# Row lists of a mixture of experts: tokens outside an expert numbered from the end, twelve of sixteen tiles listed in the first part

## The reference

```python
logits = tokens @ router_weight.T + router_bias        # 2048 tokens, 8 experts
top, experts = top_k(logits, 4); share = softmax(top)  # 4 experts for each token
for e in range(8):                                     # rows = the tokens that chose e
    gate, up = rows @ gate_up_proj[e].T + gate_up_bias[e]
    y = (limited up + 1) * glu(gate) @ down_proj[e].T + down_bias[e]
    out[rows] += share[rows, e] * y
```

## Time and profile before

| | |
|---|---|
| median of 3 runs | 985.96 us (985.22 to 992.37) |
| profiled execution | 991.85 us, of which 990.1 us from its first to its last instruction |
| mean granted TensorE clock | 0.880 |
| PE, DVE, ACT, POOL busy | 82%, 64%, 50%, 29% of the span |
| first part | ends at 617.3 us of the span |
| second part | 617.8 to 990.1 us |

### The profile page before, as it was taken

How to read it: one execution, slowest core, us unless ns; L and a number is a source line. 1 busy time by engine, 2 the same in 40 slices (tenths; PEclk the granted TensorE clock), 3 DMA queues, 4 the chain that set the end, 5 groups by cost and what they waited for, 6 DMA issues and landing times. The chain is left out here.

```text
span 990.1 us, 18525 instructions
## 1 busy us (share of the span) xinstructions
PE 808.7 (82%) x6324; PEld 508.7 (51%) x6324; DVE 634.9 (64%) x1238; ACT 493.2 (50%) x950; POOL 286.3 (29%) x261
## 2 busy tenths in 40 slices
PE   0682776778876888987887798899999999999993
PEld 0341332233432434432242225489899989998993
DVE  4546657787678876886779932845666666665652
ACT  1210310454353553436548572157777777777772
POOL 6005002210040100001001000236666666666643
PEclk9796688759997997987867799789999999999997
DMA  8421362014230161102544311314444444444432
GB/s 279 115 67 57 110 182 79 32 44 129 49 113 33 37 194 34 49 23 96 178 144 139 120 64 43 109 34 66 67 67 66 66 67 67 66 67 66 65 47 32
DMA packets 72072, 83.22 MB, mean 84 GB/s; under 512 B 10288, under 2 KB 65200, under 8 KB 71856
## 3 DMA queue, kind: packets, MB, share of 16 engines
q1 hardware_dynamic: 57008, 61.25, 20.3%
q0 software_dynamic: 14976, 20.78, 13.0%
HBM read 52.71 MB, written 29.29 MB: 83 GB/s over the span
## 5 line engine op out<-in xcount | busy, mean ns | idle before, releaser
L1600 PE MATMUL gu_ps<-xt,w 128*128 128x256 f16 x1872 | 219.6, 275 | 1.2 <-ACT xt L1321 1.2
L672 ACT ACTIVATE p<-st 128x512 f32<-128x512 f32 x256 | 139.1, 597 | 137.9 <-PE st L1156 137.1
L883 DVE TENSOR_REDUCE neg_max<-sc 128x2 f32<-128x1024 f32 x128 | 156.5, 1222 | 61.9 <-PE sc L1132 60.6
L1600 PEld LDWEIGHTS gu_ps<-xt,w 128*128 (+1 forms) x1872 | 182.6, 99 | 23.6 <-issue 1.9
L1391 POOL DMA_INDIRECT out<-y,block_rows x78 | 125.4, 1608 | 103.4 <-ACT y L1351 83.0
L1614 PE MATMUL dn_ps<-w,h 128*128 (+1 forms) x936 | 108.6, 273 | 0.3 <-DVE h L1518 0.3
L1383 POOL DMA_INDIRECT gx<-xr_d,block_rows x78 | 86.0, 1102 | 51.5 <-DVE block_rows L1491 28.6
L1132 PE MATMUL sc<-kz,sq 48*128 48x512 f16 x256 | 61.9, 453 | 45.9 <-DVE neg_max L883 41.4
L1614 PEld LDWEIGHTS dn_ps<-w,h 128*128 128x128 f16 x936 | 91.5, 98 | 11.2 <-issue 0.6
L580 POOL COPY rden_rows<-rden 128x512 f32<-128x512 f32 x16 | 10.7, 668 | 282.3 <-DVE rden L904 250.1
L1509 DVE TENSOR_SCALAR up<-up 128x512 f32<-128x512 f32 x78 | 33.4, 428 | 83.0 <-ACT up L1337 82.9
(11 more groups left out here) (200 smaller groups left out, 1108.6 us busy)
## 6 DMA issues: line engine op xcount, KB each, us to landing
stack_d<-t SPq DMA_DIRECT2D x16, 256.0 KB, 2.4
raw<-in_gate_up_t SPq DMA_DIRECT2D x4, 1024.0 KB, 5.2
raw_next<-in_gate_up_t SPq DMA_DIRECT2D x4, 1024.0 KB, 5.5
sq<-stack_d SPq DMA_DIRECT2D x16, 192.0 KB, 3.6
kz<-stack_d SPq DMA_DIRECT2D x16, 192.0 KB, 4.7
sq<-stack_d SPq DMA_DIRECT2D x32, 96.0 KB, 2.4
kz<-stack_d SPq DMA_DIRECT2D x32, 96.0 KB, 2.3
ctx_pad<-in_ctx SPq DMA_DIRECT2D x4, 512.0 KB, 4.3
```

Source lines behind the costliest of these rows:

```text
L672: act.activation(p32[:, n // 2 % RING, 2 * (n % 2) + i, :], st[:, i, :], ACT.Exp, scale=QSCALE).then_inc(s_exp, 1)
L883: dve.tensor_reduce(neg_max[:, qt, :, pair], sc[:], AX.X, ALU.max, negate=True).then_inc(m_max, 1)
L1600: ins = pe.matmul(gu_ps[:, 2 * half + g, q * ROWS:(q + 1) * ROWS], weights(i, wi, slice(col, col + P)), xt[:, i % 2, kd, xi, :], start=(j ...
```

## The change

Tokens outside an expert are now numbered from the end of the 2048 places: such a token's place is 2047 minus the number of unchosen tokens ahead of it, and that needs no count of the expert. `behind` holds the token's number minus 2047. All places can be made before the later tiles are chosen, so the lists of the first twelve tiles (`FIRST` = 12) are made in the first part, in seven new steps of batch 3. The last four tiles (`T` = 4) stay in the second part. `base` holds the counts of the first twelve tiles; `take_rows` adds the two lists. `chosen` becomes float16, and the constants come in one transfer `list_no` of 128 x 3456 float16 (864 KB) into `raw`, once the weights of expert 6 are split. In the first part `low_hot` has room for four experts (`LOW_HOT`), in `raw_next`, so the step `list_low(7)` waits for the matmuls `list_rows(3)`. In the second part the transfers `high_no` and `low_no` (512 KB each) are gone, all experts' lists are listed ahead of `gate_up(0, 0)`, and DVE does the last `take_rows` and `list_rows` 2 to 4 ahead of `unit(0)`. The fillers ahead of the last `den`, `den_turn` and `o_proj` are gone; other counts of fillers are cut. `den_turn` has the same condition as `den`.

```diff
+HI = B * S // P
+FIRST = NT - T
+LIST_NO = (("low_no", (P, FIRST)), ("high_no", (HI, E * FIRST)), ("lower", (P,)), ("ones", (P,)), ("token", (E * FIRST,)),
+           ("token_last", (E * T,)))
+MIDDLE = (P - 1) / 2
...
+    parts["high_token"] = room(HI * E * FIRST // 2).bitcast(F16).rearrange("p (h x) -> p h x", h=HI)
+    parts["rows_first"] = room(E * HI)
+    parts["place"], parts["high"], parts["unchosen"] = (by_tile(room(E * FIRST)) for _ in range(3))
+    parts["high16"], parts["low16"] = (by_tile(room(E * FIRST // 2).bitcast(F16)) for _ in range(2))
+    parts["low_hot"] = raw_next[:].bitcast(F16).rearrange("p (n l t) -> p n l t", l=P, t=FIRST)
...
+            def list_load(b, _):
+                sp.wait_ge(w_lo, (E - 1) * WP)
+                sp.dma_start(lists["numbers"], t["list_no"]).then_inc(list_in, 16)
...
+            def list_place(b, _):
+                done, _ = counted(list_step, 0)
+                pre = sc[:, 1, 0:E * (FIRST + 1)].rearrange("p (e t) -> p e t", e=E)
+                dve.wait_ge(list_pre, 1)
+                done(dve.tensor_copy(base[:], pre[:, :, FIRST]))
+                done(dve.scalar_tensor_tensor(lists["unchosen"], chosen[:, :, 0:FIRST], -1.0,
+                                              route_const["behind"][:, None, 0:FIRST].to_broadcast([P, E, FIRST]), ALU.add, ALU.mult))
+                done(dve.scalar_tensor_tensor(lists["place"], pre[:, :, 0:FIRST], -MIDDLE, lists["unchosen"], ALU.add, ALU.add))
+                done(dve.tensor_scalar(lists["high"], lists["place"], 1 / P, ROUND, ALU.mult, ALU.add))
+                done(dve.tensor_scalar(lists["high16"], lists["high"], ROUND, None, ALU.subtract))
+                done(dve.scalar_tensor_tensor(lists["low16"], lists["high16"], -float(P), lists["place"], ALU.mult, ALU.add))
+
+            def list_high(b, _):
+                done, _ = counted(list_step, 6)
+                over = lambda a: a[:, None, :].to_broadcast([P, HI, E * FIRST])
+                dve.wait_ge(list_in, 16)
+                done(dve.tensor_tensor(lists["high_token"], lists["high_no"], over(lists["high16"].rearrange("p e t -> p (e t)")), ALU.is_equal))
+                done(dve.tensor_tensor(lists["high_token"], lists["high_token"], over(lists["token"]), ALU.mult))
+
+            def list_low_(b, e):
+                need(dve, list_mm, e - LOW_HOT + 1)
+                dve.tensor_tensor(lists["low_hot"][:, e % LOW_HOT], lists["low_no"],
+                                  lists["low16"][:, e, None, :].to_broadcast([P, P, FIRST]), ALU.is_equal).then_inc(list_low, 1)
+
+            def list_take(b, _):
+                dve.wait_ge(list_mm, E)
+                dve.tensor_copy(lists["rows_first"], sc[:, 1, 256:256 + E * HI]).then_inc(list_took, 1)
...
             def den(b, q):
-                stay_awake(AWAKE["den"])
+                if (b, q) != (LAST, QUADS - 1):
+                    stay_awake(AWAKE["den"])
...
             def o_proj(b, u):
-                if u == 0:
-                    stay_awake(AWAKE["o_proj"])
...
+            def list_pre_(b, _):
+                pe.wait_ge(m_cp, B * QUADS)
+                pe.wait_ge(list_in, 16)
+                pe.wait_ge(choose_step, LAST * CHOOSE_STEPS)
+                pre = sc[:, 1, 0:E * (FIRST + 1)].rearrange("p (e t) -> p e t", e=E)
+                pe.matmul(pre, lists["lower"], chosen[:, :, 0:FIRST + 1], start=True, stop=False, skip_group_check=True)
+                for i in range(FIRST):
+                    ins = pe.matmul(pre[:, :, i + 1:], lists["ones"], chosen[:, :, i:i + 1].to_broadcast([P, E, FIRST - i]),
+                                    start=False, stop=(i == FIRST - 1), skip_group_check=True)
+                ins.then_inc(list_pre, 1)
+
+            def list_rows(b, e):
+                pe.wait_ge(list_low, e + 1)
+                for i in range(FIRST):
+                    ins = pe.matmul(sc[:, 1, 256 + e * HI:256 + (e + 1) * HI], lists["low_hot"][:, e % LOW_HOT, :, i],
+                                    lists["high_token"][:, :, e * FIRST + i], start=(i == 0), stop=(i == FIRST - 1))
+                ins.then_inc(list_mm, 1)
...
-            sp.dma_start(high_no, t["high_no"]).then_inc(no_in, 16)
-            sp.dma_start(low_no, t["low_no"]).then_inc(no_in, 16)
...
+            done(dve.scalar_tensor_tensor(unchosen[:], chosen[:, :, LAST], -1.0, const["behind"][:, None, LAST].to_broadcast([P, E, T]),
+                                          ALU.add, ALU.mult))
+            done(dve.scalar_tensor_tensor(unchosen[:], unchosen[:], -MIDDLE, base[:, :, None].to_broadcast([P, E, T]), ALU.add, ALU.add))
+            assert count[0] == CHOOSE_STEPS + 2
+            dve.wait_ge(pre_mm, 1)
+            done(dve.tensor_tensor(place[:], pre[:, :, 0:T], unchosen[:], ALU.add))
+            done(dve.tensor_scalar(high[:], place[:], 1 / P, ROUND, ALU.mult, ALU.add))
+            done(dve.tensor_scalar(high16[:], high[:], ROUND, None, ALU.subtract))
+            done(dve.scalar_tensor_tensor(low16[:], high16[:], -float(P), place[:], ALU.mult, ALU.add))
+            assert count[0] == PLACE_STEPS
             dve.wait_ge(rt_exp, 1)
             weigh_experts(dve, done, tmp, chosen[:, :, LAST], combine[:, LAST, :])
-            assert count[0] == CHOOSE_STEPS + WEIGH_STEPS
-
-
-            dve.wait_ge(pre_mm, 1)
-            pre = tr_ps[:, 1, 0:P].rearrange("p (e t) -> p e t", e=E)
-            dve.tensor_copy(token16[:], per_tile(const["token"]))
-            done(dve.tensor_copy(counts[:], tr_ps[:, 1, P:P + E]))
-            done(dve.scalar_tensor_tensor(after[:], pre, -1.0, per_expert(counts), ALU.mult, ALU.add))
-            done(dve.tensor_tensor(after[:], after[:], per_tile(const["token"]), ALU.add))
-            done(dve.tensor_tensor(gap[:], pre, after[:], ALU.subtract))
-            done(dve.tensor_tensor(gap[:], gap[:], chosen[:], ALU.mult))
-            done(dve.tensor_tensor(place[:], after[:], gap[:], ALU.add))
-            done(dve.tensor_scalar(high[:], flat(place), 1 / P, 0.5 / P - 0.5, ALU.mult, ALU.add))
-            done(dve.tensor_scalar(high[:], high[:], ROUND, None, ALU.add))
-            done(dve.tensor_scalar(flat(high16), high[:], ROUND, None, ALU.subtract))
-            done(dve.scalar_tensor_tensor(flat(low16), flat(high16), -float(P), flat(place), ALU.mult, ALU.add))
-            dve.wait_ge(no_in, 2 * 16)
-            done(dve.tensor_tensor(high_hot[:], high_no[:], flat(high16)[:, None, :].to_broadcast([P, HI, P]), ALU.is_equal))
-            done(dve.tensor_tensor(high_token[:], high_hot[:], flat(token16)[:, None, :].to_broadcast([P, HI, P]), ALU.mult))
+            assert count[0] == PLACE_STEPS + WEIGH_STEPS
+            done(dve.tensor_tensor(high_hot[:], lists["high_no"][:, :, 0:E * T], over(flat(high16)), ALU.is_equal))
+            done(dve.tensor_tensor(high_token[:], high_hot[:], over(lists["token_last"]), ALU.mult))
...
             def low_one_hot(e):
-                need(dve, rows_mm, e - HOT + 1)
-                dve.tensor_tensor(low_hot[:, e % HOT], low_no[:], low16[:, e, None, :].to_broadcast([P, P, NT]),
+                dve.tensor_tensor(low_hot[:, e], lists["low_no"][:, :, 0:T], low16[:, e, None, :].to_broadcast([P, P, T]),
                                   ALU.is_equal).then_inc(low_ok, 1)
...
-                dve.tensor_copy(rows[:, first * HI:last * HI], dn_ps[:, g % 2, first * HI:last * HI]).then_inc(rows_ok, 1)
+                dve.tensor_tensor(rows[:, at], dn_ps[:, g % 2, at], lists["rows_first"][:, at], ALU.add).then_inc(rows_ok, 1)
...
-            unit(0)
-            low_half(0)
             take_rows(2)
             take_rows(3)
             for i in range(2, GX + 1):
                 list_rows(i)
+            unit(0)
+            low_half(0)
...
-            pe.wait_ge(ones_m, 1)
-            pe.matmul(tr_ps[:, 0, 0:1], flat(chosen), ones[:], start=True, stop=True).then_inc(sums_mm, 1)
-            pe.matmul(tr_ps[:, 1, 0:P], const["lower"], flat(chosen), start=True, stop=False, skip_group_check=True)
-            pe.wait_ge(sums_ok, 1)
-            pe.matmul(tr_ps[:, 1, 0:P], tile_sums[:], const["tiles_before"][:, 0:P], start=False, stop=True, skip_group_check=True)
-            pe.matmul(tr_ps[:, 1, P:P + E], tile_sums[:], const["tiles_before"][:, P:], start=True, stop=True,
-                      skip_group_check=True).then_inc(pre_mm, 1)
+            pre = tr_ps[:, 0, 0:E * (T + 1)].rearrange("p (e t) -> p e t", e=E)
+            pe.matmul(pre, lists["lower"], chosen[:, :, FIRST:], start=True, stop=False, skip_group_check=True)
+            for i in range(T):
+                ins = pe.matmul(pre[:, :, i + 1:], lists["ones"], chosen[:, :, FIRST + i:FIRST + i + 1].to_broadcast([P, E, T - i]),
+                                start=False, stop=(i == T - 1), skip_group_check=True)
+            ins.then_inc(pre_mm, 1)
...
-            list_expert(2)
-            list_expert(3)
+            for e in range(2, E):
```

(19 more changed lines are left out.)

91 lines of the change are left out of this document (50 added, 41 removed).

## The result

Both kernels ran in turn on one chip, 20 times each. The kernel before had a median of 991.32 us (984.24 to 995.27), the changed one 984.29 us (978.35 to 989.84). The ratio is 0.995 with a 95% interval of 0.9928 to 0.9972: faster by 5.0 us, with 2.8 to 7.1 in the interval. The two medians lie 7.0 us apart and the two means 5.7. The executions of before fall into two groups, nine from 984.2 to 987.3 and eleven from 990.5 to 995.3, and their median sits at the edge of the upper one, so of the three figures the medians' difference is the weakest.

The account below looks back on a forecast made before the run. The 46.6 us before 664.4 were read as a chain over DVE, POOL and PE, later time as PE's. Gain 10.75 less loss 4.05 is 6.7 us, off 985.96: 979.3 us; range 975.5 to 985.5, own range 977.5 to 981.5.

Parts of the forecast that it names:

- First part, +4.05 us: Loss from steps added to the first part: `list_pre` 0.45, `list_rows` 0.3, late `o_add(1)` 1.6, clock fall 1.7 us.
- the stretch up to `o_proj`: First part ahead of `o_proj`: `list_pre` costs 0.45 us, `list_rows` 1 and 2 in place of six fillers 0.3.
- Up to `gate_up(0, 0)`, 5.9 us: Second part to its first block: shorter lists and an earlier gather start `gate_up(0, 0)` at 635.0 instead of 640.88.
- To `gate_up(1, 0)`, 10.0 us: From `gate_up(0, 0)` to `gate_up(1, 0)`: ACT comes last, 10.0 us instead of 12.66, gain 2.65.
- `gate_up(1, 0)` to `gate_up(2, 0)`, 2.2 us gained: Second part, between these blocks: 8.7 us at full clock instead of 10.93; 1.7 of the gain is the clock.
- the second fall of the clock: Rival: clock falls again while PE waits for `take_x(1)`; gain 5.0 us, time 981.0, chance 0.22.
- The base: Starting time for the whole kernel: median of the runs, 985.96 us, rather than the profiled execution of 991.85.
- The bound of 1%: Whole kernel: a measurement tells about 1% (9.9 us) from no change; chance of landing within it 0.88.
- Slow one-hots: Rival: DVE runs one-hots with short rows at the float32 rate; gain 3.1 us, time 982.9, chance 0.08.
- Late constants: Rival: the constants' transfer lands late, costing from 9 us of landing on; 12 us gives 982.3; chance 0.02.
- Half clock to the end of the first part: Slower rival: clock at half from before `o_proj` to that end; -1.2 us gain, time 987.2, chance 0.04.
- More gained: Rival: no clock fall and most of `list_low(7)` covered in the first part; gain 10.0 us, time 976.0, chance 0.06.

Follow-up runs that it names:

- fillers_back: Changed kernel with the 3, 6 and 3 removed fillers back ahead of the last `den`, `den_turn` and `o_proj`; profiled execution 981.15 us.
- low_early: Changed kernel with expert 3's one-hot ahead of `o_norm` and its list ahead of `o_proj`, one-hots 4 to 7 right behind `o_norm`; profiled execution 979.75 us.
- gate_fillers: Changed kernel with ten fillers in PE's pause between `turn_x(1)` and `gate_up(1, 0)`; profiled execution 983.47 us.

## Why the prediction was right or wrong

- **First part, +4.05 us: measured +4.39, and for the reasons given.** Of `list_pre` twelve matmuls took 0.54 us and the first lay mostly beside them (0.45 predicted). Three one-hots in 2.69 us, so 0.89 each. `o_proj` 1.57 us longer (1.7), `o_add(1)` 1.48 us later against the end of `o_proj` (1.6). The term that was too small is the stretch up to `o_proj`: 1.30 us in all instead of 0.75, because the clock fell at 586.6, ahead of `den_turn`, whose matmuls took 1.09 us instead of 0.60. `list_rows` 1 and 2 ran at half clock too, but in 1.59 us, as in fillers_back at full clock (1.58). fillers_back shows the cause, low_early the place of `o_add(1)`.
- **Up to `gate_up(0, 0)`, 5.9 us: measured 5.57.** First gather 8.95 us after the start of the part (9 to 10), block 17.47 (17.2). The missed term is the clock again: I let it hold through the pause ahead of `turn4`, as in the earlier trace rows. It fell at 610.5, the eight fillers took 3.57 us, and the prefix sums, which the prediction had "ready before they are asked for", came 0.65 us late. In low_early, where the clock held there, `gate_up(0, 0)` starts 0.62 us earlier (16.85).
- **To `gate_up(1, 0)`, 10.0 us: measured 10.03.** ACT came last, as said.
- **`gate_up(1, 0)` to `gate_up(2, 0)`, 2.2 us gained: measured 0.95 (1.03 against the second profile of before). This is the step that failed: "at full clock 3 x 2.62 for the matmuls".** The prediction named the second fall of the clock as a rival, with 981.0 us and 1.7 us as its price, and chose against it. It came, with the 24 matmuls in 4.46 us, and gate_fillers puts its price at 1.67 us. The case for the choice was one pause of 2.5 us without a fall in the earlier trace rows. In both profiles of the changed kernel both pauses of 2.5 us were followed by one; with the first part of before the pause ahead of `turn4` was not, in any of four profiles. Twenty fillers stand ahead of that pause where before had thirty; no run put them back, so what made the difference there stays open. The pause ahead of `gate_up(1, 0)`, behind other work, was followed by a fall in one kernel and not in the other (low_early held through 2.08 us, fillers_back fell behind 2.17), so its length alone did not decide, and one row that held was weak evidence.
- **The sum.** 6.7 us were predicted and 4.8 to 6.0 measured by the stages, 5.0 by the ratio; the rival's sum of 5.0 was nearer. The interval of the ratio, 2.8 to 7.1, holds both sums, so it is the stages that decide between them. The fall at 624.1, over `gate_up(0, 0)`, stood in no term; the stage behind it came as forecast (10.03), and no run tried to keep the clock up there.
- **The base: the larger part of the error in the time.** 979.3 was 985.96 less 6.7. But 985.96 is the median of three executions of a kernel whose executions scatter from 984.2 to 995.3; over 20 it is 991.32. The profiled execution of 991.85 us, which I called near the highest, was an ordinary one. With the same sum and that base the forecast would be 984.6; that the median of 984.29 comes so near to it is luck, since the medians' difference of 7.0 us hides what the stages say of the sum. The measured 984.29 lies outside the forecast's own range (977.5 to 981.5), and within that of 975.5 to 985.5 only because this was wide.
- **The bound of 1%.** The change is within 1%, as forecast, but the sentence that a measurement tells about 1% from no change was too coarse, and with it the choice to count a gain of 6.7 us as none: twenty alternating executions of each gave an interval of ±0.22%, wholly on the faster side, and told 0.5% from nothing.
- **The others.** Slow one-hots: no; 512 elements took 0.42 us and 1536 took 0.96, the fast rate also with rows of 4 and 12. Late constants: no, 4.6 us. Half clock to the end of the first part: no, it was back at 593.1. More gained: no.

## What to carry to other kernels

Where fillers keep the clock up, a change that shortens the work between them moves every pause, so each pause of PE after the change is to be priced both ways, with a fall (here 0.6 to 1.7 us each) and without; the fillers that prevent a fall can eat most of what they save (ahead of `o_proj` 1.12 of 1.58 us), and they are free where PE waits for another engine anyway (gate_fillers). An operation that is put into a gap of DVE is not free if it reads two inputs from SBUF while POOL works on the path, nor if it waits for PE and stands ahead of what everybody waits for. When runs of a kernel scatter by more than the change is worth, cut the traces at common events and sum the stages: here they repeat to 0.02 us, where the clock falls at the same places, while the whole moves by 9.
